# Mixture-of-experts stage of a graph kernel: the experts with an odd number walk their chunks of 256 rows downwards

## The reference, cut to what matters

```
h     = layernorm(x1)                                  # x1 = x + graph convolution
idx   = argmax(softmax(h @ gate_w + gate_b))           # one expert for each token
pos   = number of earlier tokens with the same expert;   kept = pos < 1954
hid   = relu(h[tokens of e] @ w1[e] + b1[e])           # 256 -> 1024
y     = (hid @ w2[e] + b2[e]) * prob * kept            # 1024 -> 256
out   = x1 + y
```

## Time and profile before

| | us |
|---|---|
| timed, median of 3 runs | 2517.27 (2515.47 to 2517.34) |
| profiled execution, its own time | 2514.71 |
| its span, first to last instruction | 2513.2 |
| start of the expert stage's gathers (L729) | 1788.57 |
| last matmul of the expert stage starts its group | 2479.20 |
| last scatter (L740) starts | 2502.78 |

### The profile page before, as it was taken

One profiled execution on the slowest core, in us unless ns is written; L12 is line 12 of the kernel. 1 busy time (PEld: TensorE's weight loads), 2 busy tenths in 40 slices (PEclk: granted clock), 3 DMA queues, 4 the chain that ended last, 5 costly groups with the idle time before them and its releaser, 6 DMA issues. The chain is left out here.

```text
span 2513.2 us, 36856 instructions
## 1 busy us (share of the span) xinstructions
PE 1964.8 (78%) x11102; PEld 1697.2 (68%) x11102; DVE 1313.4 (52%) x3826; ACT 1009.5 (40%) x1897; POOL 1513.9 (60%) x1612
## 2 busy tenths in 40 slices
PE   3016778866876786887878889998699999999995
PEld 2005556755765675775767789887588788788874
DVE  7987874455245335345152358877444444445443
ACT  1577654355435435435253234342233323232332
POOL 6734777777777777777777777774223523422234
PEclk8557889988998998998989889999699999999998
DMA  9236335733663573663747779787313212212211
GB/s 264 76 107 202 106 105 181 236 105 105 208 209 105 180 235 106 200 215 117 258 147 235 219 209 240 217 233 178 93 37 73 85 34 75 74 39 69 62 49 29
DMA packets 235523, 359.07 MB, mean 143 GB/s; under 512 B 46584, under 2 KB 172696, under 8 KB 235220
## 3 DMA queue, kind: packets, MB, share of 16 engines
q0 software_dynamic: 74176, 194.10, 26.8%
q1 hardware_dynamic: 159860, 160.86, 21.0%
q10 hardware_dynamic: 1312, 2.10, 0.3%
HBM read 305.38 MB, written 56.40 MB: 144 GB/s over the span
## 5 line engine op out<-in xcount | busy, mean ns | idle before, releaser
L680 POOL DMA_INDIRECT arena<-z_table,arena x1216 | 1150.3, 946 | 434.4 <-issue 360.1
L1818 PE MATMUL bank<-arena 128*128 128x128 f32 x4864 | 708.8, 307 | 239.1 <-DMA arena<-z_table,arena 121.0
L1818 PEld LDWEIGHTS bank<-arena 128*128 128x128 f32 x4864 | 660.3, 217 | 333.6 <-issue 252.9
L1276 DVE TENSOR_TENSOR nodes<-nodes,bank 128x256 f32 x304 | 127.7, 420 | 696.1 <-PE bank L1818 676.5
L740 POOL DMA_INDIRECT out<-arena x128 | 130.2, 1017 | 410.8 <-DVE arena L1690 388.3
L2059 PE MATMUL bank<-arena 128*128 128x256 f32 (+1 forms) x1472 | 329.0, 383 | 9.1 <-DVE arena L1638 9.1
L943 ACT ACTIVATE nodes<-bank,arena 128x256 f32<-128x256 f32 (+1 forms) x368 | 152.4, 465 | 451.6 <-PE bank L2059 451.6
L2071 PE MATMUL bank<-arena,nodes 128*128 128x256 f32 (+1 forms) x1472 | 326.0, 379 | 0.0
L2059 PEld LDWEIGHTS bank<-arena 128*128 128x128 f32 x1472 | 281.8, 195 | 49.9 <-DVE arena L1638 11.7
L827 ACT ACTIVATE arena<-iota_h,arena 128x490 f16<-128x490 f16 x280 | 194.7, 695 | 290.2 <-PE bank L1830 290.0
L2071 PEld LDWEIGHTS bank<-arena,nodes 128*128 128x128 f32 (+1 forms) x1472 | 272.6, 187 | 40.1 <-issue 1.0
(11 more groups left out here) (321 smaller groups left out, 1881.3 us busy)
## 6 DMA issues: line engine op xcount, KB each, us to landing
arena<-z_table SPq DMA_DIRECT2D x96, 768.0 KB, 4.7
arena<-z_table,arena POOLq DMA_INDIRECT x1216
arena<-in_L_ffn_w SPq DMA_DIRECT2D x14, 1024.0 KB, 8.8
z_table<-nodes SPq DMA_DIRECT2D x14, 896.0 KB, 9.3
x_rows<-nodes SPq DMA_DIRECT2D x98, 128.0 KB
arena<-in_x SPq DMA_DIRECT2D x48, 256.0 KB, 3.1
out<-nodes SPq DMA_DIRECT2D x96, 128.0 KB
nodes<-in_x SPq DMA_DIRECT2D x12, 896.0 KB, 11.6
```

Of the source, the lines that this page charges most:

```text
L680: nc.gpsimd.indirect_dma_start(gath[:, slot, t, :], None, z_table, bass.IndirectOffsetOnAxis(ap=src_idx[:, tile_at:tile_at + 1], axis=0)). ...
L1818: last = nc.tensor.matmul(agg_bank[i % AB][:, k * P:(k + 1) * P], gath[:, i, t, k * P:(k + 1) * P], sel[:, i, t, :], start=(t == 0), stop= ...
```

## The change

A function `chunk_of(s)` gives the chunk of an expert that position s works on. In the first expert of each pair (even number) it is chunk s, as before. In the second (odd number) it is chunk 7 - (s - 8): the expert starts with its last chunk, of 162 rows, and ends with chunk 0. Gathers and scatters, branches, and row counts all use it. An odd expert now has its empty chunks first, so PE waits for the weights at every live position of an odd expert (`if s % NCH == 0 or j`), and the branch for an empty position of an odd expert now holds a turn of the next chunk, with its own branch. Nothing is added or taken away otherwise: the same 64 positions, 8 for each expert, in the same order of experts.

```diff
--- before.py
+++ after.py
@@ -179,9 +179,13 @@
     NCH = -(-CAP // CR)
     CHUNKS = [(c, min(CR, CAP - c)) for c in range(0, CAP, CR)]
     PC = 2 * NCH
+
+    def chunk_of(s):
+        return CHUNKS[s % NCH] if s // NCH % 2 == 0 else CHUNKS[NCH - 1 - s % NCH]
+
     XSLOTS = 8
     FB2 = FT // 2
-    assert PC % XSLOTS == 0 and NCH % 2 == 0 and FB2 == 4 and KD == 2
+    assert CT == 2 * NCH and PC % XSLOTS == 0 and NCH % 2 == 0 and FB2 == 4 and KD == 2
     ARENA = 20096
 
     ctx = ExitStack()
@@ -725,7 +729,8 @@
                     pool.wait_ge(S["res_ok"], 2 * (n - XSLOTS) + 4)
                     pool.wait_ge(S["xh_ok"], 2 * (n - XSLOTS) + 2)
                 for t in range(2):
-                    rows = list_i[:, 2 * n + t:2 * n + t + 1]
+                    column = n // NCH * CT + chunk_of(n)[0] // P + t
+                    rows = list_i[:, column:column + 1]
                     nc.gpsimd.indirect_dma_start(xs_rows[:, slot, t, :], None, x_rows,
                                                  bass.IndirectOffsetOnAxis(ap=rows, axis=0)).then_inc(S[f"xs_in{slot}"], 16)
             for n in range(FETCH):
@@ -735,7 +740,7 @@
                 if n + FETCH < NE * NCH:
                     fetch(n + FETCH)
                 for t in range(2):
-                    m, slot = min(P, CHUNKS[n % NCH][1] - t * P), n % 2 * 2 + t
+                    m, slot = min(P, chunk_of(n)[1] - t * P), n % 2 * 2 + t
                     pool.wait_ge(S["res_ok"], 2 * n + t + 3)
                     nc.gpsimd.indirect_dma_start(
                         out, bass.IndirectOffsetOnAxis(ap=out_idx[0:m, 2 * n + t:2 * n + t + 1], axis=0), o_tile[0:m, slot, :], None,
@@ -930,13 +935,13 @@
                 act.sem_inc(S["tick"], 1)
                 for j in range(2):
                     for c in range(NCH):
-                        n, s = CHUNKS[c][1], j * NCH + c
+                        n, s = chunk_of(j * NCH + c)[1], j * NCH + c
                         if c == 1 and q * 2 + j + 2 < NE:
                             all_took.append(rows_of(q * 2 + j + 2))
                         if s + 1 < PC:
                             norm_rows(q, s + 1)
                             act.sem_inc(S["tick"], 1)
-                        with act.If(all_took[q * 2 + j] > CHUNKS[c][0]):
+                        with act.If(all_took[q * 2 + j] > chunk_of(s)[0]):
                             act.wait_ge(S["l2_ps"], q * (2 * PC) + (2 * s + 2))
                             for f in range(FT):
                                 act.wait_ge(S["l1_ps"], q * (PC * FB2) + ((s + 2) * FB2 + f // 2 + 1))
@@ -1631,8 +1636,8 @@
 
             def feats(q, s, took):
 
-                n = CHUNKS[s % NCH][1]
-                with dve.If(took > CHUNKS[s % NCH][0]):
+                n = chunk_of(s)[1]
+                with dve.If(took > chunk_of(s)[0]):
                     dve.wait_ge(S["xT_ps"], q * PC + (s + 2))
                     dve.wait_ge(S["l1_ps"], q * (PC * FB2) + (s + 1) * FB2)
                     nc.vector.tensor_copy(xs_feat[:, s % 2, :, 0:n],
@@ -1653,10 +1658,10 @@
 
             def results(q, s, took):
 
-                j, c = s // NCH, s % NCH
-                with dve.If(took > CHUNKS[c][0]):
+                j = s // NCH
+                with dve.If(took > chunk_of(s)[0]):
                     for t in range(2):
-                        n, slot = min(P, CHUNKS[c][1] - t * P), s % 2 * 2 + t
+                        n, slot = min(P, chunk_of(s)[1] - t * P), s % 2 * 2 + t
                         token = xs_rows[0:n, s % XSLOTS, t, :]
                         at_step = [0]
 
@@ -2047,9 +2052,9 @@
                 pe.sem_inc(S["xT_ps"], 1)
 
             def up(q, s):
-                j, n = s // NCH, CHUNKS[s % NCH][1]
+                j, n = s // NCH, chunk_of(s)[1]
                 pe.wait_ge(S["xT_ok"], q * PC + (s + 3))
-                if s % NCH == 0:
+                if s % NCH == 0 or j:
                     pe.wait_ge(S[f"w_in{j}"], q * 32 + 32)
                 for b in range(FB2):
                     pe.wait_ge(S["hid_ok"], q * (PC * FT) + (s * FT + 2 * b + 2))
@@ -2079,7 +2084,7 @@
             pe.sem_inc(S["l2_ps"], 2)
 
             def turn_or_skip(q, s, took):
-                with pe.If(took > CHUNKS[s % NCH][0]):
+                with pe.If(took > chunk_of(s)[0]):
                     turn_chunk(q, s)
                 with pe.Else():
                     skip_turn(q, s)
@@ -2089,7 +2094,7 @@
                 took = all_took[2 * q:2 * q + 3]
                 for s in range(PC):
                     inside = s % NCH < NCH - 1
-                    with pe.If(took[s // NCH] > CHUNKS[s % NCH][0]):
+                    with pe.If(took[s // NCH] > chunk_of(s)[0]):
                         up(q, s)
                         if inside:
                             turn_or_skip(q, s + 1, took[s // NCH])
@@ -2098,8 +2103,10 @@
                         pe.wait_ge(S["l2_ps"], q * (2 * PC) + (2 * s + 2))
                         pe.sem_inc(S["l1_ps"], FB2)
                         pe.sem_inc(S["l2_ps"], 2)
-                        if inside:
+                        if inside and s < NCH:
                             skip_turn(q, s + 1)
+                        elif inside:
+                            turn_or_skip(q, s + 1, took[1])
                     if not inside:
                         turn_or_skip(q, s + 1, took[(s + 1) // NCH])
```

## The result

| | before | after |
|---|---|---|
| timed, median of 5 runs each | 2517.27 (2515.47 to 2519.12) | 2528.03 (2524.65 to 2529.47) |
| ratio, 95% interval | | 1.0043 (1.0031 to 1.0054) |
| profiled execution | 2514.71 | 2529.47 |
| its span | 2513.2 | 2528.0 |
| start of the first down (position 0) | 1807.07 | 1811.91 |

The kernel is 0.43% slower, 10.8 us by the medians. Of the 14.8 us between the two profiled spans 4.8 were there before the first down, in the part that the change does not touch. The expert stage itself lost 10.0.

The account below looks back on a forecast made before the run. PE was taken as the bound, busy 665.66 of 700.30 us, then a 26.9 us tail without PE. +9.4 + 11.2 - 6.8 = +13.8 on 2514.71 gave 2528.5, timed 2531.1, stated 2530.5; range 2523 to 2538.

Parts of the forecast that it names:

- Tail and last run: Empty positions 52 to 60 and kernel end: PE waits for position 61's gather, one scatter pair follows the last down; +9.4 us.
- Run 6 to 11: Six empty positions, experts 0 to 1: PE waits for position 12's gather, landing in 6.3 us beside weights; +11.2 us.
- Border 1 to 2: Experts 1 to 2: no empty position left between them, 1.76 us in place of 8.59; -6.8 us.
- Borders 2 to 3 and 3 to 4: Three empty positions move from experts 3 to 4 to experts 2 to 3, at equal cost; 0, with 0.7 us either way.
- At nothing: Other expert borders, expert 5's moved short chunk, added weight waits and the longer empty-position branch: all taken as costing nothing.
- The added waits and branches: PE's waits for weights and longer branch at odd experts: hidden, taken as nothing; upper bound for exposed jumps 13 us.
- Expert 5's short chunk: Moves from the end of expert 5 to its start; taken as no change.
- POOL's backlog: Behind each long empty run: position 62's gather comes 5.3 us after 61's, hidden by 2 us; without that cover up to 5.
- Rival (a): Positions 12 and 61: look-ahead covers the long runs, DVE's skips end them; -13.2 us, 2504.1; chance 0.06.
- Rival (b): Both long empty runs: part of the new wait is smaller, gathers in quiet, warmer restarts; 2524.1; chance 0.10 for below 2525.
- (c): PE at live positions of odd experts: the longer branches show; +13 us more, 2543; chance 0.04.
- (d): Behind each long empty run: POOL's backlog opens a second gap, 3 to 5 us each; 2534 to 2540; chance 0.12.

Follow-up runs that it names:

- Expert 7 alone: Kernel before with the added code, but only expert 7 walks its chunks downwards, experts 1, 3 and 5 upwards; ratio 1.0036 to the kernel before.
- the run with late weights: Changed kernel, but SP loads the weights of experts 2, 4 and 6 five positions later; ratio 1.0021 to the kernel before.
- the run with the code alone: Changed kernel with odd experts walking upwards again, added waits for weights and longer branch for empty positions kept; ratio 0.9995 to the kernel before.
- the run with twelve ahead: Changed kernel with 16 slots and gathers twelve positions ahead instead of six; 2509.93 us, ratio 0.9964 to the kernel before.
- four ahead: Kernel before, old order, with gathers four positions ahead instead of six; ratio 1.0058 to the kernel before.

## Why the prediction was right

The mechanism is the one stated: both turns stand where they were expected (33.7 and 20.7 behind the down, for some 34 and 21), released by ACT's norm, with POOL never idle for more than 0.31 us up to the last gather, and one pair of scatters behind the last down. The time, 2528.03, is 2.5 below the 2530.5 stated, and inside the range. The sum of the expert stage was +13.8, measured +10.0, so it was 3.8 too high. That the time came closer than the sum is chance: the timed medians lie 10.8 apart, not 10.0, and the 2530.5 was stated 0.6 below what the sum gave.

- **Tail and last run, +9.4.** Measured 94.2 - 86.3 = +7.9 from the down of position 51 to the end. POOL's 18.22 us were exact. The price of the run was 30.5 for 31.6 to 31.7: the landing was 3.6, not 4.0, landing to up 3.1, not 3.4, and up to down took 2478.59 - 2469.42 = 9.17, not 9.6. The down of position 63 came 13.8 behind that of 62, where I had 14.25; the last position of an expert has no turn ahead of its down, and the old trace had this too (2479.20 - 2465.38 = 13.82). The last scatter starts 10.7 behind its down, as before. Expert 7 alone shows the whole of it at one place.
- **Run 6 to 11, +11.2.** Measured 18.0 - 7.2 = +10.8. The landing of 6.3 beside the weights was exact, in part by luck: the gather at 1803.56, from which I took it as one of tokens, is the first of position 6, behind expert 0's 1306 tokens, and reads the spare row alone. Gathers of tokens beside the first load of weights (1798.55 and 1799.81) took 6.2 and 6.5. The run with late weights shows that the weights made 3.3 of the 6.3. By the fit in the Trainium skill (DMA: Bandwidth & Descriptors, Anatomy of one DMA), an estimated 2.3 whatever else runs, the price would have been lower still than the 14.6 measured in quiet, where the landing was 3.0; the measurement decides against using it here.
- **Border 1 to 2, -6.8.** Measured 1.5 - 8.6 = -7.1.
- **Borders 2 to 3 and 3 to 4, 0.** Measured (8.3 + 1.5) - (1.8 + 9.4) = -1.3. I had 0, with 0.7 either way; only the tail and last run was off by more (1.5). Against the 9.2 worked out, the restart went at 2092.91 - 2083.78 = 9.1 where 9.6 was taken, the turn came 10.7 behind the down where I had taken 11.7 from a run of four at another place, and up came 2.8 behind the turn, not 2.1. A run of three inside a pair had no row of its own.
- **At nothing.** The added waits and branches: zero for runs of up to four, by the run with the code alone, and hidden behind the gathers in the two long runs. Expert 5's short chunk: -0.3 with the two borders around it (from the down of expert 4's last position to expert 6's first, 128.98 against 129.32). POOL's backlog did not show: ACT had done the norm of position 62 by 2471.93 and then waited 1.3 us for PE, so this was the cover, not the 2 us worked out (there I had let the ReLUs run ahead of the up that feeds them). The downs behind both runs keep their usual 14.25 and 13.82.
- **Rival (a)** was refuted for this kernel by the releasers, and the run with twelve ahead built its condition. Its mechanism then held only in part: freed of the gathers, the runs stopped at 13.7 and 18.9 and not at the 10.6 and 12.6 that DVE's skips would give, since PE took longer to pass empty positions than that. I had read DVE as the end of every short run and had not asked when PE itself would come. This would have cost rival (a) some 9 us had it been the case.
- **Rival (b)** held for the last run alone, whose price was 1.1 lower than stated; position 12's gather did stand beside the weights, and its restart took 9.58. **Rivals (c), (d)** did not occur.

The kernel before and the new one lie 4.8 us apart before the first down, with the same code. That is as large as half of the effect. What made the steps checkable was the distance from down to down, which repeats to 0.01 us for plain positions (14.25 or 14.26, 27 times in either kernel).

## What to carry to other kernels

Where one engine takes part in every step, empty or not, and runs a fixed number of steps ahead, its cost stays hidden only for runs of empty steps shorter than its look-ahead; an order that gathers the empty steps in one place turns hidden cost into waiting. Count the longest run against the look-ahead before reordering. Here this is shown by runs of six and nine with six ahead, and of four with four ahead; a run of three with four ahead was hidden, and the run of nine was hidden with twelve. Once the look-ahead is longer than the run, the same order can win, as it did here by 0.4% through its shorter tail. What then ends the run is the next engine that passes the empty steps one by one, here PE.

## What the runs showed of the hardware

- A branch over the code of an empty position is not free on PE. In the run with twelve ahead PE reached position 61's turn at 2448.86, 13.9 us after the end of its last down (2428.00 + 6.91), having passed nine empty positions: 1.5 us each on average, in steps of 0.8 to 3.6 us where ACT's norms show them. With four of them passed in one branch it took 2441.64 - 2430.23 = 11.4. In the kernel before, four empty positions took at most 4.8 us (2438.66 - 2426.92 - 6.91), 1.2 each. Whether the time goes to fetching instructions behind the jump was not tried.
- A gather of 128 rows mostly landed in 2.7 to 3.0 us in quiet when the rows were tokens and in 3.6 to 4.3 when all 128 indices named the one spare row. The two gathers of position 12, issued from 0.3 us before the load of expert 2's weights to 1.1 us behind it, took 6.1 and 7.1 in the kernel before and 5.7 and 6.3 in the new one. That many equal indices are slower was not separated by a run of its own.
- PE's restart did not cost more after a longer idle time: behind idle times of 3.5 to 26.7 us, in all runs, up to down took 8.9 to 10.5 us against 7.35 in steady work. The three idle times of 26.6 to 26.7 us were followed by 9.2, 9.1 and 9.9. In the stretch 2469.42 to 2478.10 the granted clock, the third number from the end, was 0.80:

```profile
2469.42:2478.10 8.68, 8.68 (x32) 7.38 (x33) 0.00 (x0) 3.61 (x8) 6.85 (x7) 0.80 0.20 48
```
